# Preparing the first four input groups of each FFN in four tiles, with a PSUM bank for each half of their output projection

## The reference, cut to what matters

```
x = x + 0.5 * ffn(layernorm(x))
x = x + attn(layernorm(x))      # attn itself adds its own input: y + cfc(ssm(norm(y))) @ out_w.T + out_b
x = x + 0.5 * ffn(layernorm(x))

ffn(x): h = bit_linear(x, w1)            # 1024 -> 4096
        h = depthwise_conv1d(h, 3 taps) + bias
        return bit_linear(silu(h), w2)   # 4096 -> 1024
bit_linear(x, w): x is rounded to 8 bits with one scale per row (127 / max|x|),
                  w to -1, 0, 1 with one scale for the matrix
cfc: h_t = ff1 * (1 - t) + t * ff2, with three gates of the input and h_(t-1), 512 wide
```

## Time and profile before

| what | value |
|---|---|
| runs | 1721.22, 1722.78, 1829.82 us; median 1722.78 us |
| profiled execution | 1719.35 us, span 1717.8 us on the slowest core (core 6) |
| spans of the eight cores | 1714.5 to 1717.8 us, granted clock 0.944 to 0.951 |
| first head (core 6) | first transfer issued 186.05 us, first L587 at 223.21 us |
| second head | first output projection at 1084.68 us, first L587 at 1134.18 us |
| busy | PE 74%, DVE 68%, ACT 56%, POOL 37% of the span |

### The profile page before, as it was taken

How to read it: one execution, slowest core, us unless ns; L and a number is a source line. 1 busy time by engine, 2 the same in 40 slices (tenths; PEclk the granted TensorE clock), 3 DMA queues, 4 the chain that set the end, 5 groups by cost and what they waited for, 6 DMA issues and landing times. The chain is left out here.

```text
span 1717.8 us, 29950 instructions; the slowest of 8 cores (1714.5 to 1717.8 us)
## 1 busy us (share of the span) xinstructions
PE 1279.5 (74%) x9089; PEld 860.0 (50%) x9107; DVE 1172.6 (68%) x2126; ACT 958.1 (56%) x1428; POOL 642.6 (37%) x668
## 2 busy tenths in 40 slices
PE   0000087698898998998659987357699999998999
PEld 0000065465565665654348866135465655655644
DVE  4898568687687776774266666458776776777741
ACT  0426167766776766674246654146666666665651
POOL 0000322555756746547500024221633535334332
PEclk9999999899999999999869999579999999998999
DMA  9590210212122221114120000111111111200111
GB/s 290 176 334 4 62 38 13 62 37 51 38 50 62 62 51 38 51 38 118 55 50 2 2 1 2 52 59 50 50 50 64 61 50 56 81 26 26 50 38 62
DMA packets 35765, 105.66 MB, mean 62 GB/s; under 512 B 4756, under 2 KB 14100, under 8 KB 34584
## 3 DMA queue, kind: packets, MB, share of 16 engines
q1 hardware_dynamic: 24568, 95.08, 16.7%
q0 software_dynamic: 11040, 8.66, 3.5%
HBM read 84.58 MB, written 25.70 MB: 64 GB/s over the span
## 5 line engine op out<-in xcount | busy, mean ns | idle before, releaser
L587 PE MATMUL bank<-xqT,w1q 128*128 128x258 bf16 (+1 forms) x4352 | 575.4, 277 | 111.2 <-DVE y L891 110.6
L587 PEld LDWEIGHTS bank<-xqT,w1q 128*128 128x128 fp8e4 x4352 | 417.4, 100 | 277.4 <-issue 149.3
L608 PE MATMUL bank<-w2q,q 128*128 128x512 fp8e4 x2112 | 535.2, 383 | 0.0
L921 DVE SCALAR_TENSOR_TENSOR y<-bank,convws,y 128x256 f32<-128x256 f32 (+1 forms) x544 | 256.4, 471 | 270.3 <-ACT y L738 269.2
L1055 POOL TENSOR_TENSOR y<-y,Rb 128x1024 f32<-128x1024 f32 (+1 forms) x136 | 322.8, 2403 | 179.3 <-ACT Rb L763 179.3
L738 ACT ACTIVATE y<-bank,convbs,convws 128x256 f32<-128x256 f32 (+1 forms) x544 | 293.1, 551 | 165.0 <-PE bank L587 161.3
L608 PEld LDWEIGHTS bank<-w2q,q 128*128 128x128 f16 x2112 | 206.1, 98 | 166.1 <-issue 7.9
L891 DVE SCALAR_TENSOR_TENSOR y<-bank,convws,y 128x256 f32<-128x256 f32 (+1 forms) x544 | 253.8, 467 | 0.1
L689 ACT ACTIVATE y<-y 128x1024 f32<-128x1024 f32 (+1 forms) x136 | 139.9, 1029 | 149.5 <-DVE y L891 149.3
L832 DVE TENSOR_TENSOR M<-M,ab 128x1024 f32<-128x1024 f32 (+1 forms) x119 | 199.4, 1676 | 2.2 <-ACT ab L701 2.2
L711 ACT ACTIVATE q<-y,qoff 128x1024 f16<-128x1024 f32 (+1 forms) x136 | 151.8, 1117 | 65.8 <-POOL y L1055 62.3
(11 more groups left out here) (159 smaller groups left out, 1328.7 us busy)
## 6 DMA issues: line engine op xcount, KB each, us to landing
raw<-w1T SPq DMA_DIRECT2D x8, 2048.0 KB, 35.2
raw<-w2T SPq DMA_DIRECT2D x8, 2048.0 KB, 17.8
xg<-xall SPq DMA_DIRECT2D x18, 512.0 KB, 5.2
x1t<-xall SPq DMA_DIRECT2D x17, 512.0 KB, 4.1
basebuf<-x1t SPq DMA_DIRECT2D x17, 512.0 KB, 3.1
xg<-basebuf SPq DMA_DIRECT2D x16, 512.0 KB, 4.6
x2buf<-xg SPq DMA_DIRECT2D x16, 512.0 KB, 2.9
x1t<-x2buf SPq DMA_DIRECT2D x16, 512.0 KB, 4.3
```

The lines of the kernel that those rows point to most:

```text
L587: mm = pe.matmul(pA[n % 4][:, 0:tw + 2], w1q[:, c, k * P:(k + 1) * P], xqT[j % 3][:, c, 0:tw + 2], start=c == 0, stop=c == DC - 1)
L608: pe.matmul(pB[e % 2][:], q[:, qs, kh, :], w2q[:, kh, 512 * h:512 * h + 512], start=kh == 0, stop=False)
L921: dve.scalar_tensor_tensor(v, pA[n % 4][:, 0:tw], convws[:, 3 * k:3 * k + 1], v, ALU.mult, ALU.add).then_inc(conv1_done, 1)
```

## The change

Four tiles serve the head: `xg[0]`, `xg[1]`, and for groups 2 and 3 `x1t[0]`, `x1t[1]`, which are not needed before the first `res_load`. All four loads are issued at once. In the second FFN each of the eight half projections has a bank of its own (the four `pA`, the two `pB`, `pM`, `pT`), and PE waits once, for all eight additions, before its first transpose. DVE takes the additions and the statistics of all four groups first. `coef_x` does two groups in one pass in the head (two columns instead of one), and everywhere it has six operations instead of seven: `center` is now `(xg - mean) * rs`. The head's quantisation moves from POOL to DVE (`quant_head`), and ACT's and DVE's lists for the head have another order. The per-group scalars have four places instead of two, so some waits in the tile loop are for older groups. The bias rows are loaded to the place of `xqT` instead of to `x1t[0]`.

In the cut diff below, `...` stands for lines that change only names (`xg[g % 2]` to `xbuf(g)`, `g % 2` to `g % 4`) or not at all.

```diff
--- before.py
+++ after.py
@@ tiles and counters @@
+    ob32 = at('ob32', XQT, [P, D])
...
-    pmv = small('pmv', 4)
-    pco = small('pco', 4)
-    ptm = small('ptm', 2)
+    pmv = small('pmv', 8)
+    pco = small('pco', 8)
+    ptm = small('ptm', 4)
     pam = small('pam', 1)
-    psc = small('psc', 4)
+    psc = small('psc', 8)
...
+    xh_in = [sem('xh_in0'), sem('xh_in1')]
+    xh_out = [sem('xh_out0'), sem('xh_out1')]
...
+    def xbuf(g):
+        return x1t[g - 2] if g in (2, 3) else xg[g % 2]
+    def x_in(g):
+        return xh_in[g - 2] if g in (2, 3) else xg_in[g % 2]
+    def x2_stored(g):
+        return xh_out[g - 2] if g in (2, 3) else x2_out[g % 2]
+    def x_turn(g):
+        return 1 if g < 4 else g // 2
...
+    def out_bank(g, h):
+        return (pA + pB + [pM, pT])[2 * g + h] if g < 4 else pM
...
@@ x_load @@
-        if g >= 2:
-            sp.wait_ge(xq_done, g - 1)
+        if g >= 4:
+            sp.wait_ge(xq_done, g - 3 if g < 6 else g - 1)
@@ res_load @@
         if m >= 2:
             sp.wait_ge(st_out[m % 2], 16 * (m // 2))
+        else:
+            sp.wait_ge(xq_done, m + 3)
@@ ffn_sp @@
-        for gg in (0, 2):
-            x_load(ph, xw, gg)
-            x_load(ph, xw, gg + 1)
-            if ph == 2:
-                x2_store(gg)
-                x2_store(gg + 1)
+        for g in range(4):
+            x_load(ph, xw, g)
+        if ph == 2:
+            for g in range(4):
+                x2_store(g)
         x_load(ph, xw, 4)
@@ ffn_pe: project_out and the head @@
-            if pm_val:
+            if g >= 4 and pm_val:
                 pe.wait_ge(pm_sem, pm_val)
+            dst = out_bank(g, h)
             for b in range(KC):
-                pe.matmul(pM[0:n, :], hC[:, b, P * g:P * g + n], ow[:, b, 512 * h:512 * h + 512], start=b == 0, stop=False)
+                pe.matmul(dst[0:n, :], hC[:, b, P * g:P * g + n], ow[:, b, 512 * h:512 * h + 512], start=b == 0, stop=False)
...
-        for gg in (0, 2):
-            if ph == 2:
-                project_out(gg, 0)
-                project_out(gg, 1)
-                project_out(gg + 1, 0)
-                project_out(gg + 1, 1)
-            turn_x(gg)
-            turn_x(gg + 1)
+        if ph == 2:
+            for g in range(4):
+                project_out(g, 0)
+                project_out(g, 1)
+            pe.wait_ge(opadd_done, 8)
+        for g in range(4):
+            turn_x(g)
@@ ffn_act: the head @@
-        for gg in (0, 2):
-            round_x(gg)
-            round_x(gg + 1)
-            place_x(gg)
-            place_x(gg + 1)
+        round_x(0)
+        round_x(1)
+        place_x(0)
+        place_x(1)
+        round_x(2)
+        place_x(2)
+        round_x(3)
+        place_x(3)
@@ ffn_dve: stat_x, amax_x, the head @@
-            if g >= 2:
-                dve.wait_ge(pcoef_done, g - 1)
+            if g >= 4:
+                dve.wait_ge(xc_done, g - 3)
...
-            if g >= 2:
-                dve.wait_ge(xq_done, g - 1)
+            if g >= 4:
+                dve.wait_ge(xq_done, g - 3)
...
-        for gg in (0, 2):
-            for g in (gg, gg + 1):
-                if ph == 2:
-                    add_out(g, 0)
-                    add_out(g, 1)
-                stat_x(g)
-            amax_x(gg)
-            amax_x(gg + 1)
+        def quant_head(g):
+            dve.wait_ge(rnd_done, g + 1)
+            if g:
+                dve.wait_ge(pT_done, g)
+            dve.tensor_scalar(xqb[:], xbuf(g)[:], SHIFT, psc[:, 2 * g:2 * g + 1], ALU.add, ALU.mult).then_inc(xq_done, 1)
+
+        for g in range(4):
+            if ph == 2:
+                add_out(g, 0)
+                add_out(g, 1)
+            stat_x(g)
+        amax_x(0)
+        amax_x(1)
+        quant_head(0)
+        quant_head(1)
+        amax_x(2)
+        quant_head(2)
+        amax_x(3)
+        quant_head(3)
@@ ffn_pool: coef_x, center, the head @@
-        def coef_x(g):
+        def coef_x(g, c=1):
...
-            pool.wait_ge(pstat_done, g + 1)
-            if g >= 2:
-                pool.wait_ge(xc_done, g - 1)
+            pool.wait_ge(pstat_done, g + c)
+            if g >= 4:
+                pool.wait_ge(xc_done, g - 3)
...
-            pool.tensor_tensor(rs, rs, tm, ALU.mult).then_inc(pcoef_part, 1)
-            pool.wait_ge(pcoef_part, n_pc + 6)
-            pool.tensor_scalar(pco[0:n, a + 1:a + 2], pmv[0:n, a:a + 1], rs, -1.0, ALU.mult, ALU.mult).then_inc(pcoef_done, 1)
-            n_pc += 6
+            pool.tensor_tensor(rs, rs, tm, ALU.mult).then_inc(pcoef_done, c)
+            n_pc += 5
...
-            pool.tensor_scalar(xg[g % 2][0:n, :], xg[g % 2][0:n, :], pco[0:n, a:a + 1], pco[0:n, a + 1:a + 2],
-                               ALU.mult, ALU.add).then_inc(xc_done, 1)
+            pool.tensor_scalar(xbuf(g)[0:n, :], xbuf(g)[0:n, :], pmv[0:n, a:a + 1], pco[0:n, a:a + 1],
+                               ALU.subtract, ALU.mult).then_inc(xc_done, 1)
...
-        for gg in (0, 2):
-            coef_x(gg)
-            center(gg)
-            coef_x(gg + 1)
-            center(gg + 1)
-            quant_x(gg)
-            quant_x(gg + 1)
+        for g in (0, 2):
+            coef_x(g, 2)
+            center(g)
+            center(g + 1)
@@ cfc_pool @@
-        pool.dma_start(x1t[0][0:1, :], obr).then_inc(ob_in, 16)
-        pool.dma_start(x1t[0][32:33, :], obr).then_inc(ob_in, 16)
+        pool.dma_start(ob32[0:1, :], obr).then_inc(ob_in, 16)
+        pool.dma_start(ob32[32:33, :], obr).then_inc(ob_in, 16)
```

More of the change, by code:

```diff
@@ L463, in x2_store @@
         sp.wait_ge(opadd_done, 2 * g + 2)
-        sp.dma_start(x2buf[P * g:P * g + n, :], xg[g % 2][0:n, :]).then_inc(x2_out[g % 2], 16)
+        sp.dma_start(x2buf[P * g:P * g + n, :], xbuf(g)[0:n, :]).then_inc(x2_stored(g), 16)
     def res_load(ph, xw, m):
@@ L472, in res_load @@
         else:
-            sp.wait_ge(x2_out[m % 2], 16 * (m // 2 + 1))
-            sp.wait_ge(x2_out[(m + 1) % 2], 16 * ((m + 1) // 2 + 1))
+            sp.wait_ge(x2_stored(m), 16 * x_turn(m))
+            sp.wait_ge(x2_stored(m + 1), 16 * x_turn(m + 1))
             sp.dma_start(x1t[m % 2][:], x2buf[P * m + 1:P * m + 1 + P, :]).then_inc(xr_in[m % 2], 16)
@@ L560, in project_out @@
                 pe.wait_ge(ob_split, 4)
-            if pm_val:
+            if g >= 4 and pm_val:
                 pe.wait_ge(pm_sem, pm_val)
+            dst = out_bank(g, h)
             for b in range(KC):
-                pe.matmul(pM[0:n, :], hC[:, b, P * g:P * g + n], ow[:, b, 512 * h:512 * h + 512], start=b == 0, stop=False)
-            pe.matmul(pM[0:n, :], sel[:, 0:n], obhl[:, 512 * h:512 * h + 512], start=False, stop=True).then_inc(op_done, 1)
-            pm_sem, pm_val = opadd_done, 2 * g + h + 1
-        for gg in (0, 2):
-            if ph == 2:
-                project_out(gg, 0)
-                project_out(gg, 1)
-                project_out(gg + 1, 0)
-                project_out(gg + 1, 1)
-            turn_x(gg)
-            turn_x(gg + 1)
+                pe.matmul(dst[0:n, :], hC[:, b, P * g:P * g + n], ow[:, b, 512 * h:512 * h + 512], start=b == 0, stop=False)
+            pe.matmul(dst[0:n, :], sel[:, 0:n], obhl[:, 512 * h:512 * h + 512], start=False, stop=True).then_inc(op_done, 1)
+            if dst is pM:
+                pm_sem, pm_val = opadd_done, 2 * g + h + 1
+        if ph == 2:
[5 more added lines that the diff above has]
+            turn_x(g)
         for j in range(nt + 2):
@@ L665, in round_x @@
             n = rows(ph, g)
-            act.activation(xg[g % 2][0:n, :], xg[g % 2][0:n, :], AF.Identity, bias=cmag[0:n, :],
-                           scale=psc[0:n, 2 * (g % 2) + 1:2 * (g % 2) + 2]).then_inc(rnd_done, 1)
+            a = 2 * (g % 4)
+            act.activation(xbuf(g)[0:n, :], xbuf(g)[0:n, :], AF.Identity, bias=cmag[0:n, :], scale=psc[0:n, a + 1:a + 2]).then_inc(rnd_done, 1)
         def place_x(g):
@@ L783, in add_out @@
             if h == 0:
-                dve.wait_ge(xg_in[g % 2], 16 * (g // 2 + 1))
-            v = xg[g % 2][0:n, 512 * h:512 * h + 512]
-            dve.tensor_tensor(v, pM[0:n, :], v, ALU.add).then_inc(opadd_done, 1)
+                dve.wait_ge(x_in(g), 16 * x_turn(g))
+            v = xbuf(g)[0:n, 512 * h:512 * h + 512]
+            dve.tensor_tensor(v, out_bank(g, h)[0:n, :], v, ALU.add).then_inc(opadd_done, 1)
         def stat_x(g):
@@ L1018, in quant_x @@
             n = rows(ph, g)
-            a = 2 * (g % 2)
+            a = 2 * (g % 4)
             pool.wait_ge(rnd_done, g + 1)
@@ L1022, in quant_x @@
                 pool.wait_ge(pT_done, g)
-            pool.tensor_scalar(xqb[0:n, :], xg[g % 2][0:n, :], SHIFT, psc[0:n, a:a + 1], ALU.add, ALU.mult).then_inc(xq_done, 1)
+            pool.tensor_scalar(xqb[0:n, :], xbuf(g)[0:n, :], SHIFT, psc[0:n, a:a + 1], ALU.add, ALU.mult).then_inc(xq_done, 1)
         def coef_out(m):
```

30 lines of the change are left out of this document (15 added, 15 removed).

## The result

| | time, us | runs |
|---|---|---|
| before | 1721.22 (1719.57 to 1829.82) | 19 |
| after | 1733.91 (1729.87 to 1821.12) | 19 |
| forecast | 1699.3 (1692 to 1711) | |

The change makes the kernel **slower**: ratio (after to before) 1.0086, 95% interval 1.0063 to 1.0109, 12.7 us by the medians. The forecast was a gain of 23.5 us; its sign is wrong and the time lies outside its range. In some executions of every kernel half of the cores shows a lower granted clock and takes longer: ratios, intervals and the times of the experiments leave such runs out, the ranges in this table hold them, and the profiled execution after (1744.12 us) has a mild form of it, with spans of 1726.7 us on cores 0 to 3 and 1736.8 on cores 4 to 7 (medians). Its parts are therefore somewhat too long.

The account below looks back on a forecast made before the run. It took PE as nearest to the bound overall, but each head as bound by latency through five engines; savings of 4.4 + 14.3 + 4.8 = 23.5 us from 1722.8 gave 1699.3 us, range 1692 to 1711.

Parts of the forecast that it names:

- The step that failed: POOL's centring in both heads and the loops: about 1.2 us each in the heads, no new cost in the loops.
- no gain: Rival on the heads: a wait read wrongly keeps the old order, 1718 to 1723 us; chance 0.04.
- First head: Head of the first FFN: last transposes at 218.0 instead of 222.40, 4.4 us saved.
- Second head: Head of the second FFN: projections without gaps, last transposes at 1119.1 instead of 1133.37, 14.3 us saved.
- Tile loop: Loops of both FFNs: POOL loses L993, 0.44 us in each of 11 stretches, 4.8 us saved.
- DVE's quantisation: Both heads: 0.75 us on DVE against 1.12 on POOL; the first one held by POOL's centring.
- Slower: `M` held longer: Rival in the loops: `M` waits for one more POOL operation, 2.3 us in each of 11 stretches; 1729.4 us, chance 0.06.

Follow-up runs that it names:

- e1: The changed kernel with the old centring (multiply, then add) and its seventh coefficient operation back; 1700.18 us, ratio 0.9865.
- e2: The kernel before with only the new centring (subtract, then multiply) and six coefficient operations; 1759.44 us, ratio 1.021.
- f1: The changed kernel with add-then-multiply centring, all half projections of the head in bank pM, PE waiting for each addition; 1706.32 us, ratio 0.9909.
- e3: The changed kernel with centring as add of a negated mean, then multiply, the negated mean computed off the chain; 1697.0 us, ratio 0.9844.
- f4: The kernel before with only the add-then-multiply centring, L993 off the chain; 1711.69 and 1714.03 us in two runs.
- f2: The changed kernel with add-then-multiply centring and the head's quantisation back on POOL behind the four centrings; 1700.43 us, ratio 0.9878.

## Why the prediction was wrong, point by point

**The step that failed** is the price of the centring, put at 1.2 us in the heads and at no change in the loops. It is 3.80 us (3797 ns against 1196), in all 35 centrings. The prediction took over "two centrings of 1.2 each" in the first head and "2.3 + 0.2 + 2.4" in the second, and said nothing of the centring in the loop but that its neighbour L993 goes. No sentence costs the edit from multiply and add to subtract and multiply, though the section on the change names it. It was treated as an edit with one answer, and it is an operation that the trace of before does not show. Two of the groups of wide POOL operations in before's view by lines, with their shapes kept apart (count, then busy time, mean ns, idle time):

```profile
L1162 POOL COPY hC<-hcur 128x912 bf16<-128x912 bf16 x9 | 38.0, 4227 | 165.7 <-DVE hcur L1228 126.3 <-DVE hcur L1230 39.4
...
L1010 POOL TENSOR_SCALAR xn<-x1t,mrk,mnm 128x1024 bf16<-128x1024 f32 x17 | 20.3, 1195 | 4.0 <-POOL mnm L1047 4.0
```

In the code before, every wide `tensor_scalar` of POOL has `mult` and `add` (L1002, L1010, L1015, near 1.2 us; L1023, 1.12 in the heads); none has `subtract`. And the copy, which writes every ninth element, shows that POOL can take 4.2 us for 912 columns. The bounds for the new form were therefore 1.1 and some 4.2. With the upper one the range would have reached beyond 1730, and the chance of no gain would not have been 0.04.

**What the missing term is worth.** The prediction had counted 11 stretches of the loops in which centring stands on the path. 11 x (3.797 - 1.196) = 28.6. Put into the forecast: -23.5 + 28.6 = +5.1, and with the heads, where `after` is 3.2 and 3.2 longer than `e1`, +11.5. Measured: +12.7. The heads' part of this was known only after the runs. The count of 11 is that of the trace, and it roughly holds by itself in `e2`: its loops grow by 26.3, and 28.6 less 11 x 0.44 for the missing L993 is 23.8.

**First head.** Right in size, once the centring costs 1.2: 4.4 forecast, 4.6 in `e1`, the last transposes on its core 0 at 218.01 against 218.0. That it agrees to the hundredth is luck, for on the way errors cancel. The loads did not land 2.2 apart: the third was there only by 197.80, where I had 195.4, and DVE's statistics ended 1.9 later than forecast. The first quantisation was not held on this core (0.76 us), which won 0.8 back, so the first transposes came at 206.39, 0.8 later than forecast. Then the last two sets stand 4.54 apart instead of 4.88.

**Second head.** Right: 14.3 forecast, 15.3 in `e1`. The projections run without gaps, and their clock rises on the way: on core 0 of `e1` the first three times four matmuls take 1.86, 1.32, then 1.03 us. In the window 1078 to 1096 the granted clock is 0.78 there, and it is 1.00 from 1085 to 1091; in `f1`, where PE waits before each half, it is 0.50. I had let PE rise "before it holds DVE up"; DVE waited 0.57 us once, for the second half, and then no longer for PE.

**Tile loop.** 4.8 forecast; 4.0 between `e1` and `e3`, 2.8 between before and `e3`, 6.9 in `f4`. On POOL itself the term is there: L993's 0.44 is gone from each of the 11 stretches after, and in `e3` (core 6), which has the negated mean to compute, a stretch takes 4.6 to 4.8 instead of 5.0 to 5.1, 3.9 us less in sum. How much of that reaches the time of the loops is not shown to the microsecond, since loop 2 varies by more than that on grounds that no run here isolates.

**DVE's quantisation.** 0.75 us as estimated. The first one of a head runs beside POOL's centring of groups 2 and 3: in `e1` it takes 0.75 to 1.55 us in the first head, by core, and 1.5 on every core in the second. Where DVE's took 0.76 (core 0), one of POOL's centrings took 1.72 instead of 1.19. `f2` gives the worth of the move as 2.1 and 2.8.

**The rivals.** "Slower: `M` held longer" gave 1729.4, near to the measured time, and **is not what happened**. `M` on the slowest core before (first) and after (second), in the view of one line:

```profile
L832 DVE TENSOR_TENSOR M<-M,ab x119: 681/1215/10186, 242.6 to 1658.2; 128x1024 f32<-128x1024 f32 x112, 128x512 f32<-128x512 f32 x7
```

```profile
L857 DVE TENSOR_TENSOR M<-M,ab x119: 680/1215/10172, 240.7 to 1674.8; 128x1024 f32<-128x1024 f32 x112, 128x512 f32<-128x512 f32 x7
```

On both, 28 of the 119 last longer than 2.5 us, with values that agree within 0.2 in pairs, one of them 10.2. POOL's run of four comes 2.2 us later after the statistics and `M` moved with it, 3.05 instead of 3.07. In `e3`, where the run does come earlier as the rival wants it, by 0.3 to 0.4 us, there are again 28 and the values are the same; `M` starts 4.9 to 5.3 us after the run of four in all of them. The argument against the rival was right, and its time fits by chance: a time alone confirms no mechanism. The Trainium skill (SBUF — State Buffer, Who interferes with whom) lets the loser of the shared ports wait for one instruction; the 3.05 us agree with that, the one of 10.17 beside several operations in a row doesn't, before or after. On the centring the Trainium skill (GPSIMD Engine Reference, Performance versus the Vector engine) gives a body of up to two operations 1.03 cycles an element, which makes an estimate of 0.9 us for 1024 at the 1.2 GHz that the same section uses. The 1.20 us of multiply and add are near that, the 3.80 of subtract and multiply are not.

## What to carry to other kernels

Cost every instruction whose form changes, also if its engine, tile and meaning stay: write down its operations, operands and types, look for a row with exactly that form, and where there is none bound it by the slowest wide row of the engine. An algebraic rewrite that saves a small operation can make the large one three times as long; an added `-mean` computed off the chain gave nearly the same saving without that. When a change mixes a restructuring with such a rewrite, run them apart before judging either: here one was worth 21 us and the other cost 34.
